# An LSTM of 625 steps with a cell chosen at each step: input rows added by TensorE, twelve steps of its program written out, and one of eight products of f and g for all four cells ahead of the choice

## The reference, cut to what matters

```
def _lstm_activate(gates, c):
    i, f, g, o = jnp.split(gates, 4, axis=-1)
    c_new = jax.nn.sigmoid(f) * c + jax.nn.sigmoid(i) * jnp.tanh(g)
    h_new = jax.nn.sigmoid(o) * jnp.tanh(c_new)
def step(carry, x_t):
    h, c = carry
    logits = jnp.concatenate([h, c, x_t], axis=-1) @ W_sel.T + b_sel
    onehot = jax.nn.one_hot(jnp.argmax(logits, axis=-1), 4)
    g_all = einsum('bi,sgi->bsg', x_t, W_ih) + einsum('bh,sgh->bsg', h, W_hh) + b_ih + b_hh
    g = jnp.einsum('bsg,bs->bg', g_all, onehot)
```

## Time and profile before

| what | value |
|---|---|
| median of three runs | 6272.86 us |
| profiled execution | 6278.15 us, span 6276.3 us |
| PE, PEld busy | 5392.8 us (86%), 3269.5 us (52%) |
| DVE, ACT, POOL busy | 3097.9 us (49%), 1088.6 us (17%), 612.9 us (10%) |
| mean granted clock of PE over the span | 0.944 |
| the loop of steps, 2306 to 5537 us | 3231 us |
| instruction packets on q8, all of the span | 45, 0.74 MB |

### The profile page before, as it was taken

One profiled execution on the slowest core, in us unless ns is written; L12 is line 12 of the kernel. 1 busy time (PEld: TensorE's weight loads), 2 busy tenths in 40 slices (PEclk: granted clock), 3 DMA queues, 4 the chain that ended last, 5 costly groups with the idle time before them and its releaser, 6 DMA issues. The chain is left out here.

```text
span 6276.3 us, 214043 instructions
## 1 busy us (share of the span) xinstructions
PE 5392.8 (86%) x84948; PEld 3269.5 (52%) x84948; DVE 3097.9 (49%) x13265; ACT 1088.6 (17%) x4645; POOL 612.9 (10%) x1014
## 2 busy tenths in 40 slices
PE   8998778849998929999999999999999999977778
PEld 6643443314666615555555555555555555544444
DVE  4401443214552165555555555555555555564543
ACT  0000000002331131111111111111111111122312
POOL 0000660002650000000000000000000000011100
PEclk9999998979999969999999999999999999989877
DMA  0000111467432330000000000000000000000010
GB/s 10 21 30 11 39 44 44 97 136 253 119 105 100 139 123 5 5 5 10 5 5 5 10 5 5 5 5 10 5 5 5 5 10 0 0 24 37 23 55 9
DMA packets 128787, 240.28 MB, mean 38 GB/s; under 512 B 47084, under 2 KB 64114, under 8 KB 127687
## 3 DMA queue, kind: packets, MB, share of 16 engines
q1 hardware_dynamic: 68584, 146.72, 6.6%
q0 software_dynamic: 60128, 92.58, 5.9%
HBM read 165.58 MB, written 73.29 MB: 38 GB/s over the span
## 5 line engine op out<-in xcount | busy, mean ns | idle before, releaser
L1456 PE MATMUL bank<-lstm_w,step_h_parts 128*32 128x128 f16 (+1 forms) x59904 | 1233.0, 238 | 172.1 <-issue 164.0
L1456 PEld LDWEIGHTS bank<-lstm_w,step_h_parts 128*32 128x32 f16 x59904 | 1116.8, 97 | 488.4 <-issue 478.0
L1427 PE MATMUL bank<-lstm_w 128*128 128x512 f16 x4992 | 1297.0, 383 | 3.2 <-issue 3.2
L1480 DVE TRANSPOSE_TENSOR_REDUCE step_summed<-bank 128x4 f32<-128x128 f32 x1872 | 670.0, 358 | 292.7 <-PE bank L1456 285.6
L1427 PEld LDWEIGHTS bank<-lstm_w 128*128 128x128 f16 x4992 | 386.4, 98 | 388.5 <-issue 5.1
L1406 ACT ACTIVATE step_act_out<-step_gates 128x4 f32<-128x4 f32 x625 | 128.5, 206 | 2082.3 <-DVE step_gates L1486 2078.8
L1486 DVE SCALAR_TENSOR_TENSOR step_gates<-step_summed,lstm_inv_scale,step_xgs 128x4 f32<-128x4 f32 x1872 | 416.0, 222 | 68.7
L1530 DVE COPY step_xgs<-step_xg 128x16 f32 x624 | 109.2, 175 | 688.7 <-issue 664.5
L1396 POOL COPY xnT<-step_state 128x4 f32 (+1 forms) x625 | 116.4, 186 | 3170.0 <-DVE step_state L1513 3170.0
L1109 PE MATMUL bank<-sum_parts,sum_hot 125*125 125x512 f16 x1600 | 347.6, 381 | 6.9 <-DVE sum_parts L1068 6.9
L1437 PE MATMUL bank<-lstm_wsel,step_state 128*1 128x4 f32 x4992 | 214.9, 168 | 115.3 <-DVE step_state L1503 115.3
(11 more groups left out here) (368 smaller groups left out, 6578.2 us busy)
## 6 DMA issues: line engine op xcount, KB each, us to landing
rel_h<-rel_h_sb SPq DMA_DIRECT2D x39, 1024.0 KB, 4.3
lstm_xg<-xg_g POOLq DMA_DIRECT2D x4, 5000.0 KB, 19.5
step_xg<-lstm_xg SPq DMA_DIRECT2D x25, 800.0 KB, 4.4
xg_w<-in_c_w_ih SPq DMA_DIRECT2D x8, 2048.0 KB, 10.7
lstm_w<-in_c_w_hh SPq DMA_DIRECT2D x4, 4096.0 KB, 30.8
rel_z<-rel_z_sb POOLq DMA_DIRECT2D x8, 1250.0 KB, 22.9
rel_zg<-rel_z POOLq DMA_DIRECT2D x8, 1248.0 KB
cheb_w<-in_L_gnn_weight SPq DMA_DIRECT2D x8, 1024.0 KB
```

Of the source, the lines that this page charges most:

```text
L1427: nc.tensor.matmul(idle[:], w[:, 0, 0, 0, 0, 0:128], w[:, 0, 0, 0, 0, :], start=True, stop=True)
L1456: last = nc.tensor.matmul(bank[32 * q:32 * q + 32, 0:32 * (end - first)], h_parts[:, c, :], w[:, s, c, q, a, 32 * first:32 * end], start=( ...
L1480: nc.vector.tensor_reduce(summed[:, first:end], bank[:, 0:32 * (end - first)].rearrange("p (b r) -> p b r", r=32), X_AXIS, ALU.add, apply_ ...
```

## The change

The input rows of a step are no longer added by DVE. `lstm_inputs` computes them with the time steps on partitions (125 at a time) and 512 gates of one part and cell as columns, splits each value into three bf16 parts (ACT copies the first, DVE takes the rest, ACT the second, DVE the third), and POOL stores each of the 80 tiles. The bias is kept apart in three bf16 parts. In the steps a ring of three chunks of four steps holds the parts of all cells on 48 partitions, the bias on 48 others; a product of 512 columns with 0/1 rows (times the scale) writes the input row of one gate part for all four cells into a bank (`inject`), once that bank's old sum was reduced. There are now four parts, f, g, i, o, one bank each, with four cells side by side in a bank. The products of h then add to it. One of the eight products (times four side by side) of f and of g is run for all four cells ahead of the choice (`parts_ahead`), and `cell` has 7, 7, 8 and 8 of them. The filler products go. PE's loop has 52 rounds of twelve written-out steps, each with its own four copies of `cell`. DVE reduces the chosen quarter of each bank by a register address, and ACT applies the scale in its activation. DVE's loop now begins with the choice, so that its back branch lies between the end of a step and the next maximum.

```
@@ lstm_inputs @@
+            for i in range(TILES):
+                n, m = i // NT, i % NT
+                pool.wait_ge(lo_ready, i + 1)
+                pool.dma_start(B.xg[n, :, m * R:(m + 1) * R, :].rearrange("a t g -> t a g"), parts[:, i % 4]
+                               ).then_inc(stored[i % 4], 16)
+            for k in range(4):
+                pool.wait_ge(stored[k], 16 * (TILES // 4))
...
+            def take_rest(i):
+                if i >= 4:
+                    dve.wait_ge(lo_ready, i - 3)
+                dve.wait_ge(hi_ready, i + 1)
+                nc.vector.tensor_tensor(rest[:, i % 4], B.bank[i % 6][0:R, :], parts[:, i % 4, 0], ALU.subtract
+                                        ).then_inc(rest_ready, 1)
+
+            def take_lo(i):
+                dve.wait_ge(mid_ready, i + 1)
+                nc.vector.tensor_tensor(parts[:, i % 4, 2], rest[:, i % 4], parts[:, i % 4, 1], ALU.subtract
+                                        ).then_inc(lo_ready, 1)
...
+            def keep_hi(i):
+                if i >= 4:
+                    act.wait_ge(stored[i % 4], 16 * (i // 4))
+                act.wait_ge(done, i + 1)
+                nc.scalar.copy(parts[:, i % 4, 0], B.bank[i % 6][0:R, :]).then_inc(hi_ready, 1)
+
+            def keep_mid(i):
+                act.wait_ge(rest_ready, i + 1)
+                nc.scalar.copy(parts[:, i % 4, 1], rest[:, i % 4]).then_inc(mid_ready, 1)
...
+            for i in range(TILES):
+                n, m = i // NT, i % NT
+                if m == 0:
                     pe.wait_ge(w_loaded[n % 2], 16 * (n // 2 + 1))
-                if i >= 4:
-                    pe.wait_ge(kept_a, i - 3)
-                    pe.wait_ge(kept_v, i - 3)
+                if i >= 6:
+                    pe.wait_ge(rest_ready, i - 5)
...
+                    last = nc.tensor.matmul(B.bank[i % 6][0:R, :], xnT[:, c, m * R:(m + 1) * R], w[:, n % 2, c, :],
                                             start=(c == 0), stop=(c == KC - 1))
                 last.then_inc(done, 1)
...
@@ lstm_steps @@
+    halves = [(c, a) for c in range(KC) for a in range(2)]
+    ROUNDS = (STEPS - 1) // XG_RING
...
+            def load(k, slot):
+                sp.dma_start(xg[0:XG_ROWS, slot * XG_CHUNK:(slot + 1) * XG_CHUNK, :],
+                             xg_rows[:, bass.ds(k * XG_CHUNK + 1, XG_CHUNK), :]).then_inc(xg_loaded[slot], 16)
...
+            with sp.Fori(1, ROUNDS) as r:
+                for slot in range(XG_SLOTS):
+                    sp.wait_ge(init, 1)
+                    sp.wait_ge(injected, (r * XG_SLOTS + slot - (XG_SLOTS - 1)) * XG_CHUNK)
+                    load(r * XG_SLOTS + slot, slot)
...
+                act.wait_ge(summed_f, n)
+                nc.scalar.activation(act_out[:, 0:4], summed[:, 0:4], ACT.Sigmoid, scale=L.inv[:, 0:1]
+                                     ).then_inc(sig_f, 1)
...
+            def inject(part, at, stop):
+                p, bank, _, _ = part
+                return nc.tensor.matmul(bank[:], rows[:, p, :], xg[:, at, :], start=True, stop=stop)
+
+            def add_half(part, s, c, a, stop):
+                p, bank, _, _ = part
+                for q in range(4):
+                    last = nc.tensor.matmul(bank[32 * q:32 * q + 32, 128 * s:128 * s + 128], h_parts[:, c, :],
+                                            w[:, s, c, q, a, 128 * p:128 * p + 128], start=False, stop=stop,
+                                            tile_position=(0, 32 * q))
+                return last
+
+            def cell(s):
+                for part in parts:
+                    for c, a in halves[1 if part in parts_ahead else 0:]:
+                        last = add_half(part, s, c, a, stop=(c == KC - 1 and a == 1))
+                    last.then_inc(part[2], 1)
+
+            def step(t, at):
+
+                if at % XG_CHUNK == 0:
+                    pe.wait_ge(xg_loaded[at // XG_CHUNK], 16)
+                    pe.sem_inc(xg_loaded[at // XG_CHUNK], -16)
+                for part in parts:
+                    pe.wait_ge(part[3], t)
+                    last = inject(part, at, stop=False)
+                last.then_inc(injected, 1)
...
-                keep_clock_up(WARM_PICK - 1)
-                pe.wait_ge(init, 1)
                 pe.wait_ge(h_lo_ready, t)
-                keep_clock_up(1)
+                for s in range(CELLS):
+                    for part in parts_ahead:
+                        add_half(part, s, 0, 0, stop=False)
                 pe.wait_ge(picked, 1)
                 s = pe.value_load(pick[0:1, 0:1])
...
+
+            pe.wait_ge(init, 1)
+            pe.wait_ge(rows_ready, 1)
+            pe.wait_ge(first_loaded, 32)
+            for part in parts:
+                inject(part, XG_RING, stop=True).then_inc(part[2], 1)
+            with pe.Fori(0, ROUNDS) as r:
+                for at in range(XG_RING):
+                    step(pe.snap(r * XG_RING + (at + 1)), at)
...
+            def add_rows(part, s, n):
+                p, bank, done, summed_part = part
+                nc.vector.tensor_reduce(summed[:, 4 * p:4 * p + 4], bank[:, bass.ds(s * 128, 128)].rearrange(
+                    "p (b r) -> p b r", r=32), X_AXIS, ALU.add, apply_transpose=True
+                                        )._wait_ge(done, 1).then_inc(summed_part, 1)
...
+            def parts_taken():
+                dve.sem_inc(done_f, -1)
+                dve.sem_inc(done_g, -1)
+                dve.sem_inc(done_i, -1)
+                dve.sem_inc(done_o, -1)
...
-                                      ).then_inc(xgs_ready, 1)
                 dve.sem_inc(score_done, -1)
                 dve.sem_inc(top_ready, -1)
-
-            def finish(t, n):
-
-                add_rows(part_f, t)
...
+                parts_taken()
+                return s
+
+            def finish(s, t, n):
+
+                add_rows(part_f, s, n)
+                if t is not None:
+                    dve.sem_inc(picked, -1)
+                add_rows(part_g, s, n)
                 forget(n)
-                add_input(part_ig, t)
-                add_rows(part_o, t)
+                add_rows(part_i, s, n)
+                add_rows(part_o, s, n)
                 new_i(n)
-                add_input(part_o, t)
-                dve.wait_ge(h_kept, t)
                 new_c(n)
                 weigh_h(n)
+                if t is not None:
+                    dve.wait_ge(h_kept, t)
                 new_h(n)
 
+            nc.vector.memset(xg[:], 0.0).then_inc(cleared, 1)
...
+            dve.wait_ge(rows_loaded, 16)
+            nc.vector.tensor_scalar(rows[:], rows_f[:], L.up[:, 0:1], None, ALU.mult).then_inc(rows_ready, 1)
+
+            finish(0, None, 1)
+            with dve.Fori(1, STEPS) as t:
+                s = choose(t)
+                finish(s, t, t + 1)
```

More of the change, by code:

```diff
@@ L1191, in _ @@
+            for i in range(TILES + 1):
+                if i < TILES:
+                    take_rest(i)
+                if i >= 1:
+                    take_lo(i - 1)
             dve.wait_ge(lx_done, 1)
-            nc.vector.tensor_copy(lx[:], B.bank[0][0:R, 0:NT * CELLS].rearrange("p (j s) -> p j s", j=NT)
+            nc.vector.tensor_copy(lx[:], B.bank[7][0:R, 0:NT * CELLS].rearrange("p (j s) -> p j s", j=NT)
                                   ).then_inc(lx_kept, 1)
@@ L1334, in lstm_steps @@
 def lstm_steps(nc, ctx, B, L):
+    I = B.I
     def sb(name, shape, dt):
@@ new lines, in lstm_steps @@
+    xg_loaded = [sem(f"xg_loaded{k}") for k in range(XG_SLOTS)]
+    w = L.raw[:, 0:BLOCKS, :].bitcast(F16).rearrange("p (s c q) (a k) -> p s c q a k", s=CELLS, c=KC, a=2)
+    part_f = (0, B.bank[0], done_f, summed_f)
+    part_g = (1, B.bank[1], done_g, summed_g)
+    part_i = (2, B.bank[2], done_i, summed_i)
+    part_o = (3, B.bank[3], done_o, summed_o)
+    parts = (part_f, part_g, part_i, part_o)
+    parts_ahead = (part_f, part_g)
+    score = B.bank[4][0:1, 0:8]
+    halves = [(c, a) for c in range(KC) for a in range(2)]
@@ L1423, in _ @@
         def _(pe):
-            def keep_clock_up(products):
-                for _ in range(products):
-                    nc.tensor.matmul(idle[:], w[:, 0, 0, 0, 0, 0:128], w[:, 0, 0, 0, 0, :], start=True, stop=True)
-            pe.wait_ge(init, 1)
-            with pe.Fori(1, STEPS) as t:
+            def inject(part, at, stop):
[21 more added lines that the diff above has]
+                last.then_inc(injected, 1)
                 pe.wait_ge(init, 1)
@@ L2290, in lay_out @@
         b = out.pop("L2_ffn_" + name).reshape(4, 4, 4, 4, 32)[:, order]
-        out["c_" + name] = np.ascontiguousarray(b.transpose(2, 4, 0, 1, 3).reshape(128, 64))
+        out["c_" + name] = np.ascontiguousarray(b.transpose(1, 2, 0, 3, 4).reshape(16, 512))
+    rows = np.zeros((128, 4, 128), np.float32)
+    for n in range(16):
+        rows[3 * n:3 * n + 3, n // 4, 32 * (n % 4)] = 1.0
+        rows[64 + 3 * n:64 + 3 * n + 3, n // 4, 32 * (n % 4)] = 1.0
+    out["c_xg_rows"] = rows
```

219 lines of the change are left out of this document (80 added, 139 removed).

## The result

| | before | after |
|---|---|---|
| median | 6271.5 us (6269.54 to 6273.96, 4 runs) | 11379.56 us (11368.0 to 11388.2, 4 runs) |
| span of the profiled execution, granted clock over it | 6276.3 us, 0.944 | 11366.2 us, 0.681 |
| one step of the recurrence | 5.17 us | 13.30 us |
| q8 packets in the loop, per step | 3, none | 2432, 3.90 |

The changed kernel takes 1.814 times as long (interval 1.811 to 1.818). The forecast was 10,541 us in a range of 8,300 to 12,300.

What follows compares the result with a forecast made beforehand. Bound by latency through PE, DVE and ACT in turn. Code loads on a 5.0 us path give 11.5 us a step, with the clock 12.0: 6278.15 + 4262 + 6, less 5, is 10,541 us; range 8,300 to 12,300.

Steps and rivals of the forecast that it cites:

- Rival 2: PE's loop: no code stalls, blocks stay or are fetched further ahead; 5.0 us a step, 6,175 us; chance 0.16.
- Rival 1: PE's loop: only far jumps stop PE, code in order is there when needed; 8,720 us; chance 0.11.
- Rival 3: PE's loop: no code stalls, but the clock falls without the eight fillers; 7.0 us a step, 7,420 us; chance 0.03.
- Number of loads: PE's written-out loop: code blocks loaded again in each step, 4.09 forecast.
- The walk: Stepping through PE's code addresses for 624 steps with jump odds: 3.0 blocks entered a step, 7.1 us of stops.
- The price: Time for PE to load one block of code: 3.2 us taken, with 2.8 and 3.75 as ends.
- the clock's 0.5: PE's clock in the loop: 12.0 us a step taken between 11.5 and the 12.5 at half clock all along.
- The stops: PE waiting for code: 3.6 us a step at far jumps, 3.5 entering next blocks; 7.1 in all, 0.6 of it hidden.
- The path without loads: Recurrence step through PE, DVE and ACT without code loads: 5.0 us, -0.17 against 5.17.
- Injections hidden: PE in the step: four injections of 0.21 us end before the c products behind them start, so add nothing.
- DVE's back branch: DVE's loop branch, moved between h's last part and the maximum: +0.25 us a step, between 0 and +0.39.
- Stage ahead: Input products, stores and set-up before the recurrence: together +6 us, ends -10 and +280.

Runs made afterwards that it cites:

- e1: The kernel before with only PE's loop written out for twelve steps (one filler product moved): 10,336.95 us, ratio 1.648.
- e4: The changed kernel with one step a round of PE's loop instead of twelve, ring slot from a register: 6392.86 us, ratio 1.019 to the kernel before.
- e8: Changed kernel, one PE step a round, injections behind the score, VectorE's loop written out for four steps, constant (not real) activation scale: 6274.35 us, ratio 1.0002.
- e11: e12 with VectorE's loop written out for four steps: 6054.05 us, ratio 0.965 to the kernel before.
- e2: The kernel before with PE's loop written out for two steps, about 6.6 blocks: 6278.97 us, ratio 1.0007.
- e3: The kernel before with PE's loop written out for three steps, about 9.8 blocks: 11,095.53 us, ratio 1.768.
- e10: e4 with f, g and i injected behind the cell, o behind the score, VectorE's loop written out for four steps: 6054.93 us, ratio 0.965.
- e7: e4 with the injections behind the score and no products ahead of the choice: 6370.88 us, ratio 1.0153 to the kernel before.
- e12: e7 with two filler products of 512 columns behind the cell: 6232.02 us, ratio 0.994 to the kernel before.

## Why the prediction was right, and where it was off

**The mechanism** was right: steps written out make PE load its code again in every round. e1 shows it by the length alone, e4 by its absence. Rival 2, with no stalls, falls with the first view. Rival 1, with stops at far jumps alone, falls with the 2.98 us gap in straight code, of which the 0.18 us gap of the earlier trace rows was the only sign before. There are 447 such stops of over 1 us, between two instructions of PE with no branch and no wait between them, 1.5 us a step. 344 of them are inside cells (1.2 us a step), the others in the products ahead and before the score. All 447 end 1.18 to 1.77 us after a packet of q8 has ended (median 1.38), as the misses with one packet do (1.40); e4 has one such stop in all its steps. Rival 3 is wrong as the cause (e4 has no fillers and a clock of 1.00).

That a block asks for the next one alone can be read from the packets of the kernel before. Between 2199 and 2306 us PE ran no product and q8 started no packet. In the first iteration packets start at 2309.95, 2313.79 and 2317.01. Each follows an entry into a block (2309.2, 2312.55 and 2316.25) by 0.8 to 1.2 us, and the first two end 1.35 and 1.33 us before PE goes on at 2312.55 and at 2316.25. Behind the third none comes to the loop's end.

**Number of loads:** 4.09 forecast, 3.90 measured. The walk counted a little too much: by its own chances the far jumps are 195 exits of cell 0, 0.88 of 107 exits of cell 1 and of 322 entries, and 52 back branches, 1.00 a step instead of 1.08. That makes about 3.9 loads.

**The price:** 3.2 us taken, 3.54 measured at misses with one packet, within the ends of 2.8 and 3.75. This term was mis-sized. Between the prediction's two prices, 3.54 gives 12.6 us a step, and 13.1 with the clock's 0.5, against 13.30 measured. The loads follow one another with hardly a pause: of the 2431 distances between packets 60 are over 5 us. (Their average, 3.41, is only the step's 13.30 divided by 3.90.) So the 13.1 us for loads one behind the other, which I had set above the forecast, is close to the time itself. It is no strict bound: 256 distances are under 2 us, so some loads overlap.

**The stops:** 7.1 us a step forecast. Measured: 1,016 misses, 3495 us together, 5.6 us a step, and the 1.5 in straight code, 7.1 again, though split otherwise than 3.6 and 3.5. With 1.6 misses a step against 1.0 far jumps, the entry into the next block must often fall on a branch. The agreement of the sums is partly luck, since I had more loads at fewer microseconds each and did not count the loop's branch by itself (51 misses at 4.7 us, 0.4 us a step).

**Beside the stops** stands what the forecast fell short by. It had 5.0 for the path, less 0.6 of stops hidden beside VectorE and the score, plus 0.5 for the clock: 4.9 us. Measured are 13.3 - 7.1 = 6.2, against 5.31 in e4 at full clock. Of the 0.9 between, 0.2 are stops of 0.15 to 1 us among the products with h (230 of them, none in e4). The rest holds the clock of 0.61 and shorter stops elsewhere, which no run separates. The forecast's 0.5 for the clock lies between full clock and half clock all along; half is the 0.50 of the earlier trace rows, behind the 3.6 us stop, where four fillers took 1.89 us instead of 1.04. No run shows the 0.5 by itself; the loop's clock was 0.61. That 0.6 of the stops would be hidden is not borne out.

**Signs:** 2432 packets against 2,550; medians of 3.3 and 3.7 at L1514 and L1517; from one load of the pick into PE's register to the next, steps of cell 0 to 3 take 10.6, 13.5, 14.6 and 15.3 us on average, in the order forecast (9 to 15).

**The path without loads** was wrong. I had it at 5.0 us, and e4 has 5.31. "Injections hidden" failed: I compared them with the c products, and they stood ahead of the whole score, 0.97 us from first to score. I also left out ScalarE. A gate activation took 188 to 206 ns in the kernel before and takes 205 in e8, where the scale is a constant; with the scale as a column it takes 297:

```profile
L1446 ACT ACTIVATE step_act_out<-step_summed,lstm_inv_scale x625: 297/297/299, 2326.0 to 10623.4; 128x4 f32<-128x4 f32 x157
```

DVE's back branch was forecast at +0.25, between 0 and +0.39. e11 gains 0.29 with three of four gone, which makes 0.39 for one: the upper end. Under 7 us of stops none of this could be seen.

**Stage ahead:** +6 forecast, +21 measured. The 320 products leave 640 records of PE (L1251), two passes each, as the old stage's 512 left 1,024 (L1218, L1220). The first weight reduction comes 12.8 us later (2224.4 instead of 2211.6), and what stands between it and the first step, clearing the ring and loading the biases among it, takes the other 8, as estimated. The stores did not set the pace: 80 of them at 1.29 us of POOL, 8.9 us to land, inside the +280 end.

**The size that stays:** 6.6 blocks fit (e2), 9.8 do not (e3); the runs agree with any size between. The 8 blocks in the expectations for e2 and e3 are one such size, which no run shows by itself. Loads in straight code are not hidden either: the 240 instructions of a cell take PE 1.86 us (e4), a miss takes 3.54, and 344 stops of over 1 us stand inside cells.

## What to carry to other kernels

Count the instructions of an engine's loop body before writing it out, at about 256 of PE's to a block (the mean of nine distances between packets in the kernel before). On PE a body of 6.6 blocks stayed and one of 9.8 did not; past the limit the loads came some 3.5 us apart, and the loop that was a little too long (e3) was slower than the one that was far too long (e1). Work put "in the time of a wait" is hidden only if nothing that the next engine waits for stands behind it in the same queue (in e4 the injections stood 0.97 us ahead of the score, in e10 they held it to 0.58 us behind tanh c instead of 0.35); read the order of the queue and not the idle share. Before fillers are taken away, look at the mean against the median of the period and at the granted clock (e7: 5.29 against 5.06 us, clock 0.95).

## What the runs showed of the hardware

- Once the body is past the limit, q8 loads 3.3 to 3.9 blocks a step in steady state (e1 3.32, e3 3.82, after 3.90), one every 3.4 to 3.5 us (medians); only 1.1 to 1.2 us of each is the packet.
- A missing branch back over the whole body costs more (median 4.7 us at L1530, and 4.7 in e1 and e3) than the misses within it (3.6 at L1514, 3.7 at L1515 and L1517, 3.0 at L1520).
- PE also stops in straight code for a block that is not there yet: 447 times for over 1 us (median 2.1) in 624 steps, each time until 1.18 to 1.77 us after the end of a packet of q8.
- The granted clock was 0.95 over the loop of e7, where it fell in stretches, and 1.00 in e12, which differs by two filler products of 512 columns behind the cell.
